# Query and key operands of the second attention block: turned first, split into three parts afterwards

## The chip, the cores and the metric

The kernel runs on one core of one Trainium2 chip. The metric is the time of one execution in microseconds (us) of device time; lower is better. The core has five engines with queues of their own, each worked off in order: TensorE (PE; its weight loads are shown as PEld), VectorE (DVE), ScalarE (ACT), GpSimd (POOL) and SyncE (SP, which issues DMAs here). They meet at semaphores only.

## The reference, cut to what matters

Two blocks of attention and a mixture of experts over x of shape (2, 2048, 128). The part that changes makes the operands of the second block's softmax attention:

```
xn = layernorm(x)
q = (xn @ wq.T).reshape(b, s, 16, 8);  k, v likewise
q = q * rsqrt(mean(q*q, -1) + 1e-6) * q_norm_w;   k likewise with k_norm_w
q, k = rope(q), rope(k)          # on the last 508 of 2048 positions
q = q / sqrt(8)
attn = softmax(q . k);  out = (attn @ v) @ wo.T
```

Next to it the second block's router is computed from the same xn: a softmax over 8 experts, the largest taken, and each token given a slot among the tokens sorted by expert.

## The kernel before, in words

The program is a row of stages, each a block at whose end all engines meet. The stage in question is `route_and_operands` (semaphores and buffers have the prefix `ro_`). In front of it stands a layer norm that leaves xn turned in `xnT`; behind it `sorted_experts` (`ffn_`), which needs the rows that this stage scattered; then `softmax_attention` (`at_`), whose queries and keys are loaded by DMA from what this stage leaves; then `finish`.

The stage has two halves that share the engines.

*Routing.* DVE works through a long row of small operations (L1069 to L1125), with one round trip to PE for counts (L984, L985) and one for a column sum (L987). At L1112 the slots are known; POOL then scatters 32 tiles of rows by indirect DMA (L945), and SP, which waits for all of them, loads the sorted rows (L938).

*Operands.* 4096 tokens in NG = 16 groups of 256 (TG = 2 tiles of 128). With tokens on the partitions, a group is projected (`project`, PE), its squares are taken (`square`, ACT L1007) and summed over each head (`statistics`, DVE L1133, L1135), the root is drawn (`take_root`, ACT L1016), inverted and multiplied in (`scale`, DVE L1140, L1142), groups 6, 7, 14 and 15 are rotated (`rope`, DVE L1152 to L1156), and each number is then split into three bfloat16 parts that add up to it: `first` (ACT, a copy to bfloat16), `remainder` (DVE L1160), `second` (ACT), `third` (DVE L1164). Attention wants features on the partitions, so the parts are turned by PE: `turn` (L975) makes 12 transposes of 128x128 bfloat16 for a group, 6 for queries and 6 for keys, into one PSUM bank each. `take` copies them out: queries by ACT, keys by ACT and DVE in turn. To have both plain and weighted projections the moving operand is `wqk`, 512 columns: the q and k weights, and the same times the norm weights.

The order on each engine is written by hand. PE: for g, `project(g + 2)`, then `turn(g)`, which waits for `lo` of the group (`third`), and for the bank that `take` of the group before must have emptied. ACT and DVE run loops over g in which group g is begun while groups g-1, g-2 and g-3 are at their later steps:

```
for g in range(NG + 3):          # ACT
    square(g); second(g - 2); take_values(g); first(g - 1); take_root(g); take(g - 3)
for g in range(NG + 3):          # DVE
    statistics(g); third(g - 2); scale(g); rope(g); remainder(g - 1); take(g - 3)
```

Buffers are rings of R = 3. `take_values` copies the value projection out of its bank; `project(g + 2)` waits for it and for `scale(g)`.

Of the kernel before, what the change touches and what calls it, by code (L numbers as in the profile page):

```python
# [11 lines left out]
P = 128  # L12
# [846 lines left out]

def load_rows(k, eng, U, pair, i, done):  # L860

    to = (k.queries, k.keys)[i][pair % 2]
    b, p = divmod(pair, PAIRS)
    for h in range(2):
        of = slice(2 * DK * p + DK * h, 2 * DK * p + DK * (h + 1))
        for place, part in PLACES[i]:
            at = h * HEAD_ROWS + place
            eng.dma_start(to[at:at + DK, :], U[i][of, part, b * SEQ:(b + 1) * SEQ]).then_inc(done, 16)
        if i == 0:

            at = h * HEAD_ROWS + SHIFT
            eng.dma_start(to[at:at + PARTS, :], k.zeros[0:PARTS, :].bitcast(BF16)).then_inc(done, 16)

def route_and_operands(k, w, bg, rows, r, sorted_dram, slots_of, U, V):

    nc = k.nc
# [6 lines left out]
    R = 3  # L886
    QK = 2 * D
    with ExitStack() as ctx:
# [14 lines left out]
        wqk = sb("wqk", [P, 2 * QK])  # L903
        norm = sb("norm", [P, QK])
        qk = sb("qk", [P, R, TG, QK])

        rest = sb("rest", [P, R, TG, QK])
        parts = sb("parts", [P, R, PARTS, TG, QK], BF16)
        rot = sb("rot", [P, 4, TG, 2 * HEADS, DK // 2])
# [4 lines left out]
        (weights_step, weights_made, projected, squared, summed, stat, rooted, inverted, scaled, v_out, rope_step, roped, hi, rest_out,  # L914
         mid, lo, turned, taken_q, taken_k_act, taken_k_dve) = (
            sem(n) for n in ("weights_step", "weights_made", "projected", "squared", "summed", "stat", "rooted", "inverted", "scaled",
                             "v_out", "rope_step", "roped", "hi", "rest_out", "mid", "lo", "turned", "taken_q", "taken_k_act",
                             "taken_k_dve"))
# [8 lines left out]
        weighted = lambda g: bank[:, first_bank(g):first_bank(g) + TG, QK:2 * QK]  # L927
# [20 lines left out]
        @block.tensor  # L948
        def _(pe):
            k.wait_late(pe)  # L950

            def project(g):
                if g >= 2:
                    pe.wait_ge(scaled, g - 1)
                    pe.wait_ge(v_out, g - 1)
                for t in range(TG):
                    at = g * COLS + t * P
                    nc.tensor.matmul(bank[:, first_bank(g) + t, :], xnT[:, at:at + P], wqk[:, :], start=True, stop=True)  # L958
                    mm = nc.tensor.matmul(bank[:, first_bank(g) + V_BANK, t * P:(t + 1) * P], xnT[:, at:at + P], w.wqkv[:, QK:3 * D],  # L959
                                          start=True, stop=True)  # L960
# [24 lines left out]
            nc.tensor.matmul(bank[:, COUNT_BANK, NW:2 * NW], k.ones[:, :], flat, start=True, stop=True).then_inc(counted, 1)  # L985
            pe.wait_ge(sum_ready, 1)
# [6 lines left out]
        def take_parts(copy, g, i):  # L993
            return copy(U[i][:, :, g * COLS:(g + 1) * COLS],
                        bank[:, T_BANK + i, :].bitcast(BF16)[:, 0:PARTS * COLS].rearrange("p (j t) -> p j t", j=PARTS))

        @block.scalar
        def _(act):
# [4 lines left out]
            def square(g):  # L1003
                act.wait_ge(projected, g + 1)
                if g >= R:
                    act.wait_ge(lo, g - R + 1)
                nc.scalar.activation(rest[:, g % R], plain(g), ACT.Square).then_inc(squared, 1)  # L1007
# [10 lines left out]
            def first(g):  # L1018
                act.wait_ge(scaled, g + 1)
                if turns(g):  # L1020
                    act.wait_ge(roped, turned_until(g))
                if g >= R:
                    act.wait_ge(turned, 2 * (g - R + 1))
                copy(parts[:, g % R, 0], qk[:, g % R]).then_inc(hi, 1)

            def second(g):
                act.wait_ge(rest_out, g + 1)
                copy(parts[:, g % R, 1], rest[:, g % R]).then_inc(mid, 1)

            def take(g):  # L1030
                act.wait_ge(turned, 2 * g + 1)
                take_parts(copy, g, 0).then_inc(taken_q, 1)
                if g % 2:
                    act.wait_ge(turned, 2 * g + 2)
                    take_parts(copy, g, 1).then_inc(taken_k_act, 1)

            for g in range(NG + 3):
                if g < NG:
                    square(g)
                if 2 <= g < NG + 2:  # L1040
                    second(g - 2)
                if g < NG:
                    take_values(g)
                if 1 <= g <= NG:
                    first(g - 1)
                if g < NG:
                    take_root(g)
                if g >= 3:
                    take(g - 3)

        @block.vector
        def _(dve):
# [18 lines left out]
            for i, scale in enumerate((DK ** -0.5, 1.0)):  # L1071
                ts(norm[:, i * D:(i + 1) * D].rearrange("p (h e) -> p h e", e=DK),
                   bc(w.norm_w[:, i, :].unsqueeze(1), [P, HEADS, DK]), scale, None, ALU.mult).then_inc(weights_step, 1)
# [53 lines left out]

            steps = 0

            def statistics(g):  # L1130
                dve.wait_ge(squared, g + 1)
                total = st[:, g % R, 0]
                red(total, by_head(rest[:, g % R]), X_AXIS, ALU.add).then_inc(summed, 1)  # L1133
# [3 lines left out]
            def scale(g):  # L1137
# [4 lines left out]
                tt(by_head(qk[:, g % R]), by_head(weighted(g)), bc(rstd.unsqueeze(3), [P, TG, 2 * HEADS, DK]), ALU.mult).then_inc(scaled, 1)  # L1142

            def rope(g):
                nonlocal steps
                dve.wait_ge(scaled, g + 1)
                a = by_head(qk[:, g % R])
                x0, x1 = a[:, :, :, 0:DK:2], a[:, :, :, 1:DK:2]
                at = g % ROPED * TG
                cos, sin = (bc(f[:, at:at + TG, :].unsqueeze(2), [P, TG, 2 * HEADS, DK // 2]) for f in (w.cos, w.sin))  # L1150
                for m, (x, f) in enumerate(((x0, cos), (x1, sin), (x0, sin), (x1, cos))):
                    tt(rot[:, m], x, f, ALU.mult).then_inc(rope_step, 1)  # L1152
                steps += 4
                dve.wait_ge(rope_step, steps)
                tt(x0, rot[:, 0], rot[:, 1], ALU.subtract)
                tt(x1, rot[:, 2], rot[:, 3], ALU.add).then_inc(roped, 1)  # L1156

            def remainder(g):
                dve.wait_ge(hi, g + 1)
                tt(rest[:, g % R], qk[:, g % R], parts[:, g % R, 0], ALU.subtract).then_inc(rest_out, 1)  # L1160

            def third(g):
                dve.wait_ge(mid, g + 1)
                tt(parts[:, g % R, 2], rest[:, g % R], parts[:, g % R, 1], ALU.subtract).then_inc(lo, 1)  # L1164

            def take(g):
                if g % 2 == 0:
                    dve.wait_ge(turned, 2 * g + 2)
                    take_parts(cp, g, 1).then_inc(taken_k_dve, 1)

            for g in range(NG + 3):
                if g < NG:
                    statistics(g)
                if 2 <= g < NG + 2:
                    third(g - 2)
                if g < NG:
                    scale(g)
                    if turns(g):
                        rope(g)
                if 1 <= g <= NG:  # L1180
                    remainder(g - 1)
                if g >= 3:
                    take(g - 3)
# [530 lines left out]
def build(nc, a, out):  # L1714

    with ExitStack() as whole:
# [144 lines left out]
        U = [sb(whole, n, [P, PARTS, TOK], BF16) for n in ("query_parts", "key_parts")]  # L1861
# [41 lines left out]
```

## Time and the profile before

| | |
|---|---|
| Median of 3 runs | 1983.7 us (1981.62 to 1983.73) |
| The profiled execution | 1984.38 us |
| Its span, first to last instruction | 1982.3 us |
| Mean granted TensorE clock | 0.927 of 2.4 GHz |
| Stage `route_and_operands` | 419 to 574 us of the span |
| `sorted_experts` and the start of attention | 574 to 720 us |
| Softmax attention | to 1961 us |

The profile covers one execution. "Granted clock" is the share of TensorE's full speed that the throttle allowed in a stretch. In a timeline, a line is a start, a length, the engine, the line of the kernel, the operation and, in brackets, the idle time of the engine ahead of it and what ended that.

### The profile page before, as it was taken

To read this page: it belongs to the slowest core of one execution; us is meant where nothing else is said; L and a number is where in the kernel's file an instruction comes from. 1 tells how busy PE (TensorE), PEld (TensorE's weight loads), DVE (VectorE), ACT (ScalarE), POOL (GpSimd) and SP (SyncE) were. 2 spreads that over 40 slices of the span, in tenths; PEclk is the share of its full clock that TensorE was granted. 3 is DMA by queue.
4 is the path that set the end of the run, shared out by engine and by line. 5 is a ranking of instruction groups with operands and counts; after the bars stand their busy time and mean duration, and the time that the engine had idled before them with its cause. 6 is when DMAs were issued, how large, how long until landed. Compare 5 with 4: busy or idle time off the path is not lost. (4 is left out here: it accounts for less than half of the span.)

```text
span 1982.3 us, 41860 instructions
## 1 busy us (share of the span) xinstructions
PE 1718.6 (87%) x16109; PEld 717.3 (36%) x16109; DVE 1591.2 (80%) x2845; ACT 1440.3 (73%) x2873; POOL 318.5 (16%) x668
## 2 busy tenths in 40 slices
PE   4883879465669999999999999999999999999997
PEld 4453653253359422222222222222222222222224
DVE  3751435755373799999999999999999999999982
ACT  2111547423335289999999999999999999999997
POOL 2272007525030000000000000000000000002221
PEclk9896998657669699999999999999999999999998
DMA  8014111313003001010010110100101101001001
GB/s 257 17 53 113 49 49 53 92 34 86 0 2 68 18 1 18 2 18 9 11 18 1 18 18 2 18 10 10 18 3 17 18 2 18 13 6 25 16 13 52
DMA packets 64294, 61.83 MB, mean 31 GB/s; under 512 B 10752, under 2 KB 52736, under 8 KB 64096
## 3 DMA queue, kind: packets, MB, share of 16 engines
q1 hardware_dynamic: 57952, 46.56, 10.5%
q0 software_dynamic: 6144, 12.60, 2.1%
q8 instruction: 128, 2.10, 0.5%
q14 instruction: 70, 0.57, 0.1%
HBM read 23.21 MB, written 22.94 MB: 23 GB/s over the span
## 5 line engine op out<-in xcount | busy, mean ns | idle before, releaser
L1631 DVE TENSOR_REDUCE at_tops<-bank 128x1 f32<-128x512 f32 x2048 | 1234.1, 683 | 16.3 <-PE bank L1489 10.5
L1590 ACT ACTIVATE experts_then_probs<-bank 128x512 f32<-128x512 f32 x2048 | 1093.4, 600 | 75.6 <-PE bank L1509 54.9
L1509 PE MATMUL bank<-queries,keys 64*128 64x512 bf16 x2048 | 631.4, 383 | 45.3 <-ACT experts_then_probs L1590 38.4
L1489 PE MATMUL bank<-keys,queries 64*128 64x512 bf16 x2048 | 656.7, 389 | 4.9 <-POOL at_shift L1402 4.3
L1525 PE MATMUL bank<-experts_then_probs,values 128*32 128x256 f32 x8192 | 642.1, 391 | 0.0
L1509 PEld LDWEIGHTS bank<-queries,keys 64*128 64x128 bf16 x2048 | 128.4, 93 | 503.5 <-ACT experts_then_probs L1590 412.0
L1525 PEld LDWEIGHTS bank<-experts_then_probs,values 128*32 128x32 f32 x8192 | 167.9, 108 | 311.3 <-ACT experts_then_probs L1590 207.5
L1421 POOL CAST at_shift<-at_neg 128x8 bf16<-128x8 f32 x64 | 13.9, 217 | 1112.9 <-DVE at_neg L1636 1112.9
L1489 PEld LDWEIGHTS bank<-keys,queries 64*128 64x128 bf16 x2048 | 148.5, 93 | 65.7 <-DVE at_tops L1631 50.3
L653 DVE COPY ep_weights<-WB 128x642 f32 x72 | 35.8, 497 | 88.9 <-DVE ep_slots L664 46.6
L1582 ACT ACTIVATE queries<-bank 3x512 bf16<-3x512 bf16 x128 | 75.4, 589 | 32.8 <-PE bank L1499 29.5
L680 ACT ACTIVATE ep_hT<-bank,ep_weights 128x128 f32<-128x128 f32 x144 | 45.1, 365 | 48.8 <-PE bank L622 48.7
L287 POOL DMA_INDIRECT sorted_pairs<-g_rows,pair_slot x64 | 62.4, 975 | 51.3 <-DVE pair_slot L534 32.1
L1007 ACT ACTIVATE ro_rest<-bank 128x512 f32<-128x512 f32 x16 | 9.5, 596 | 81.6 <-PE bank L959 81.6
L622 PE MATMUL bank<-ep_slotsT,ep_weights 128*128 128x128 f32 x288 | 51.8, 304 | 19.3 <-DVE ep_weights L653 19.3
L975 PE MATMUL bank<-identb,ro_parts 128*128 128x128 bf16 x192 | 23.5, 294 | 51.8 <-ACT query_parts L999 38.8
L958 PE MATMUL bank<-ro_wqk,xnT 128*128 128x512 f32 x64 | 56.2, 976 | 6.9 <-DVE ro_qk L1142 4.3
L1133 DVE TENSOR_REDUCE ro_st<-ro_rest 128x64 f32<-128x512 f32 x16 | 11.0, 685 | 61.8 <-ACT ro_rest L1007 61.8
L1287 DVE COPY ffn_w<-experts_then_probs 128x512 f32 x39 | 23.2, 594 | 40.6 <-PE bank L1253 37.6
L814 DVE RECIPROCAL qg_den<-qg_den 128x512 f32<-128x512 f32 x8 | 26.8, 3353 | 34.4 <-ACT qg_den L783 34.4
L717 POOL DMA_INDIRECT g_rows<-made_of_pairs,pair_slot x32 | 31.0, 969 | 141.8 <-SPq L698 132.4
L622 PEld LDWEIGHTS bank<-ep_slotsT,ep_weights 128*128 128x128 f32 x288 | 38.4, 194 | 31.3 <-DVE ep_weights L653 29.7
(252 smaller groups left out, 1597.1 us busy)
## 6 DMA issues: line engine op xcount, KB each, us to landing
queries<-query_parts SPq DMA_DIRECT2D x192, 32.0 KB
keys<-key_parts SPq DMA_DIRECT2D x192, 32.0 KB
sorted_pairs<-zeros SPq DMA_DIRECT2D x16, 288.0 KB, 3.3
ep_slots<-sorted_pairs SPq DMA_DIRECT2D x6, 768.0 KB, 9.2
made_of_pairs<-ep_slots SPq DMA_DIRECT2D x6, 768.0 KB, 4.1
sorted_tokens<-zeros SPq DMA_DIRECT2D x8, 312.0 KB, 3.4
x<-in_L_attn_x_dram SPq DMA_DIRECT2D x4, 512.0 KB, 6.0
experts_then_probs<-in_L_ffn_W_dram SPq DMA_DIRECT2D x1, 2048.0 KB, 10.0
```

Of the source, the lines that this page charges most:

```text
L287: pool.indirect_dma_start(sorted_dram, bass.IndirectOffsetOnAxis(ap=r0.slot[i][:, t:t + 1], axis=0), rows[:, t, :], None).then_inc(scatter ...
L622: mm = nc.tensor.matmul(bank[:, H_BANK + u, i * P:(i + 1) * P], wt[:, u, i * P:(i + 1) * P], slotsT[:, j // TPC % TR, j % TPC * P:(j % TPC ...
L653: nc.vector.tensor_copy(wt[:, j % R, :], WB[:, bass.ds(at, STRIDE0)]).then_inc(w_ready, 1)
L680: nc.scalar.activation(hT[:, u, i * P:(i + 1) * P], bank[:, H_BANK + u, i * P:(i + 1) * P], ACT.Relu, bias=wt[:, u, B1_AT + i:B1_AT + i + ...
L717: pool.indirect_dma_start(y[i][:, t, :], None, made_dram, bass.IndirectOffsetOnAxis(ap=r0.slot[i][:, t:t + 1], axis=0)).then_inc(gathered[ ...
L958: nc.tensor.matmul(bank[:, first_bank(g) + t, :], xnT[:, at:at + P], wqk[:, :], start=True, stop=True)
L1489: mm = nc.tensor.matmul(bank[:, unit_bank(u) + a % WIDE, :], queries[pair % 2][rows, at:at + P], keys[pair % 2][rows, kb * CHUNK:(kb + 1) ...
L1509: nc.tensor.matmul(bank[:, bank_of("score", n, s), :], keys[pair % 2][rows, at:at + P], queries[pair % 2][rows, c * CHUNK:(c + 1) * CHUNK] ...
L1525: mm = nc.tensor.matmul(bank[32 * j:32 * j + 32, O_BANK, 0:HALF], values[pair % 2][:, kt, h, :], probs[:, s % PR, q * HALF:(q + 1) * HALF] ...
L1582: nc.scalar.activation(queries[pair % 2][rows, c * CHUNK:(c + 1) * CHUNK], bank[rows, bank_of("shifts", m), 0:HALF].bitcast(BF16), ACT.Cop ...
L1590: nc.scalar.activation(probs[:, s % PR, :], bank[:, bank_of("score", n, s), :], ACT.Exp).then_inc(p_ready, 1)
L1631: nc.vector.tensor_reduce(tops[:, m % 2, h * TPC + qt, kb // WIDE:kb // WIDE + 1], bank[:, at:at + WIDE, :].rearrange("p b n -> p (b n)"), ...
```

## The change

Only `route_and_operands` changes, and with it the layout of its result: queries and keys now share one tensor `U` of [128, 2, 3, 4096].

The step order in a group becomes: project, scale, rope, then **turn**, and the split behind it. `turn(g)` makes 4 transposes of 128x128 float32 into one bank (two banks in turn); `first`, `remainder`, `second`, `third` work on turned numbers and write straight into U, so that `take` is gone. After turning, the norm weight of a feature is one number per partition: `of_row`, [128, 2]. In groups without rotation it is multiplied in by `first` (two ACT copies of 128x256 with a scale operand) and by `remainder` (two DVE scalar_tensor_tensor of 128x256); in rotated groups it is multiplied into the cosines and sines once, in eight small DVE products (`factors`), and `rope` runs on queries and keys apart (eight products and four sums of 128x128 elements in place of four and two of 128x256). `of_row` is made by two PE transposes behind `project(0)` and `project(1)` and two DVE copies, for which DVE waits (`norm_turned`) ahead of the router's operations. The weights `wqk` and their two DVE operations are gone; the moving operand has 256 columns. PE now runs `turn(g)` ahead of `project(g + 2)`. Rings are of R = 2.

```diff
-            eng.dma_start(to[at:at + DK, :], U[i][of, part, b * SEQ:(b + 1) * SEQ]).then_inc(done, 16)
+            eng.dma_start(to[at:at + DK, :], U[of, i, part, b * SEQ:(b + 1) * SEQ]).then_inc(done, 16)
...
-    R = 3
+    R = 2
...
-                    nc.tensor.matmul(bank[:, first_bank(g) + t, :], xnT[:, at:at + P], wqk[:, :], start=True, stop=True)
+                    nc.tensor.matmul(bank[:, first_bank(g) + t, 0:QK], xnT[:, at:at + P], w.wqkv[:, 0:QK], start=True, stop=True)
...
             def turn(g):
-                pe.wait_ge(lo, g + 1)
-                for i in range(2):
-                    if g and i == 0:
-                        pe.wait_ge(taken_q, g)
-                    if g and i == 1:
-                        pe.wait_ge(taken_k_dve if g % 2 else taken_k_act, (g + 1) // 2)
-                    out = bank[:, T_BANK + i, :].bitcast(BF16)
-                    for part in range(PARTS):
-                        for t in range(TG):
-                            at = (part * TG + t) * P
-                            mm = nc.tensor.transpose(out[:, at:at + P], parts[:, g % R, part, t, i * D:(i + 1) * D], k.identb[:, :])
-                    mm.then_inc(turned, 1)
+                pe.wait_ge(scaled, g + 1)
+                if turns(g):
+                    pe.wait_ge(roped, turned_until(g))
+                if g >= 2:
+                    pe.wait_ge(hi, g - 1)
+                    pe.wait_ge(rest_out, g - 1)
+                for t in range(TG):
+                    for i in range(2):
+                        mm = nc.tensor.transpose(turned_bank(g)[:, i, t * P:(t + 1) * P], qk[:, g % R, t, i * D:(i + 1) * D], k.ident[:, :])
+                mm.then_inc(turned, 1)
...
-            pe.wait_ge(weights_made, 2)
             project(0)
             project(1)
+            pe.wait_ge(norm_made, 2)
+            for i in range(2):
+                mm = nc.tensor.transpose(bank[:, SUM_BANK, i * P:(i + 1) * P], norm[:, i * D:(i + 1) * D], k.ident[:, :])
+            mm.then_inc(norm_turned, 1)
...
             for g in range(NG):
+                turn(g)
                 if g + 2 < NG:
                     project(g + 2)
-                turn(g)
...
             def first(g):
+                act.wait_ge(turned, g + 1)
+                if turns(g):
+                    copy(of_part(g, 0), turned_bank(g)).then_inc(hi, 1)
+                else:
+                    act.wait_ge(row_step, 2)
+                    for i in range(2):
+                        ins = nc.scalar.activation(of_part(g, 0)[:, i], turned_bank(g)[:, i], ACT.Copy, scale=of_row[:, i:i + 1])
+                    ins.then_inc(hi, 1)
...
+            square(0)
+            take_values(0)
+            take_root(0)
+            for g in range(NG):
+                if g + 1 < NG:
+                    square(g + 1)
+                first(g)
+                if g + 1 < NG:
+                    take_root(g + 1)
+                second(g)
+                if g + 1 < NG:
+                    take_values(g + 1)
...
-            cp(wqk[:, 0:QK], w.wqkv[:, 0:QK]).then_inc(weights_made, 1)
-            dve.wait_ge(weights_step, 2)
-            tt(wqk[:, QK:2 * QK], w.wqkv[:, 0:QK], norm[:, :], ALU.mult).then_inc(weights_made, 1)
+            dve.wait_ge(norm_turned, 1)
+            for i in range(2):
+                cp(of_row[:, i:i + 1], bank[:, SUM_BANK, i * P:i * P + 1]).then_inc(row_step, 1)
...
+                    for m, f in enumerate((w.cos, w.sin)):
+                        tt(factors[:, i, 2 * odd + m], f[:, :, :], of, ALU.mult).then_inc(row_step, 1)
...
             def remainder(g):
                 dve.wait_ge(hi, g + 1)
-                tt(rest[:, g % R], qk[:, g % R], parts[:, g % R, 0], ALU.subtract).then_inc(rest_out, 1)
+                if g >= R:
+                    dve.wait_ge(lo, g - R + 1)
+                if turns(g):
+                    tt(rest[:, g % R], turned_bank(g), of_part(g, 0), ALU.subtract).then_inc(rest_out, 1)
+                else:
+                    for i in range(2):
+                        ins = nc.vector.scalar_tensor_tensor(rest[:, g % R, i], turned_bank(g)[:, i], of_row[:, i:i + 1], of_part(g, 0)[:, i],
+                                                             ALU.mult, ALU.subtract)
+                    ins.then_inc(rest_out, 1)
...
+            statistics(0)
+            scale(0)
+            for g in range(NG):
+                if g + 1 < NG:
+                    statistics(g + 1)
+                remainder(g)
+                if g + 1 < NG:
+                    scale(g + 1)
+                    if turns(g + 1):
+                        rope(g + 1)
+                third(g)
```

## Rows read from the trace of the kernel before

**Rows 1.** Busy time by stretch (PE, PEld, DVE, ACT, POOL; clock; DMA), the groups.

```profile
441.40:574.00 132.60, 76.98 (x304) 45.62 (x304) 65.20 (x129) 49.21 (x102) 28.51 (x29) 0.68 0.12 34
```

**Rows 2.** Waits from 418 to 575 us: total, times, longest.

```profile
ACT ro_rest L1007 <- PE bank L959: 81.6, 15, 9.2
```

**Rows 3.** Timeline of one group, 514 to 523 us.

```profile
514.63 2.02 PE L958 MATMUL bank<-ro_wqk,xnT 128*128 128x512 f32 x2
...
519.23 0.60 ACT L1007 ACTIVATE ro_rest<-bank 128x512 f32<-128x512 f32 x1 [6.95 <-PE bank L959]
...
520.69 0.69 DVE L1164 TENSOR_TENSOR ro_parts<-ro_rest,ro_parts 128x512 bf16<-128x512 f32 x1
...
521.17 0.81 ACT L999 ACTIVATE query_parts<-bank 128x768 bf16<-128x768 bf16 x1
...
522.13 1.43 PE L975 MATMUL bank<-identb,ro_parts 128*128 128x128 bf16 x12 [2.93 <-ACT query_parts L999]
```

**Rows 4.** Instructions by line and form, 418 to 575 us: busy us, mean ns.

```profile
L1142 DVE TENSOR_TENSOR ro_qk<-bank,ro_st 128x512 f32<-128x512 f32 x16 | 11.1, 692 | 0.6
...
L999 ACT ACTIVATE ro_parts<-ro_rest 128x512 bf16<-128x512 f32 x16 | 10.0, 622 | 3.5 <-DVE ro_rest L1160 3.5
...
L1140 DVE RECIPROCAL ro_st<-ro_st 128x64 f32<-128x64 f32 x16 | 8.8, 553 | 0.6 <-ACT ro_st L1016 0.6
...
L999 ACT ACTIVATE attention_values<-bank 128x256 f32<-128x256 f32 x16 | 6.0, 376 | 0.0
...
L1152 DVE TENSOR_TENSOR ro_rot<-ro_qk,cos 128x256 f32<-128x256 f32 x8 | 3.4, 422 | 0.1
...
L1096 DVE TENSOR_TENSOR ro_counts<-ro_counts 128x128 f32<-128x128 f32 x1 | 0.3, 285 | 0.0
```

**Rows 5.** Instructions by line and form of other stages, whole span.

```profile
L789 ACT ACTIVATE g_rows<-g_rows,pair_gate 128x128 f32<-128x128 f32 x32 | 10.2, 397 | 23.5 <-DMA second_rows<-made_of_pairs,pair_slot 23.5
...
L824 DVE SCALAR_TENSOR_TENSOR g_rows<-second_rows,pair_gate,g_rows 128x128 f32<-128x128 f32 x32 | 9.1, 346 | 1.1 <-ACT g_rows L789 1.1
...
L1309 ACT ACTIVATE g_rows<-bank 128x128 f32<-128x128 f32 x32 | 8.9, 277 | 10.7 <-PE bank L1253 10.7
```

**Rows 6.** Timeline of the same two lines, four in a row.

```profile
379.52 1.28 ACT L789 ACTIVATE g_rows<-g_rows,pair_gate 128x128 f32<-128x128 f32 x4 [7.76 <-DMA second_rows<-made_of_pairs,pair_slot]
379.95 1.23 DVE L824 SCALAR_TENSOR_TENSOR g_rows<-second_rows,pair_gate,g_rows 128x128 f32<-128x128 f32 x4 [1.05 <-ACT g_rows L789]
```

**Rows 7.** Timeline of the stage's start, 418 to 444 us.

```profile
421.14 0.42 DVE L1081 TENSOR_REDUCE ro_one<-ro_probs 128x32 f32<-128x256 f32 x1
...
421.34 2.05 PE L958 MATMUL bank<-ro_wqk,xnT 128*128 128x512 f32 x2 [2.60 <-DVE ro_wqk L1079]
...
426.88 1.28 ACT L1016 ACT_TABLE_LOAD   x1
...
429.55 0.42 DVE L1092 COPY ro_counts<-bank 128x256 f32<-128x256 f32 x1 [4.85 <-PE bank L985]
...
441.38 0.68 DVE L1133 TENSOR_REDUCE ro_st<-ro_rest 128x64 f32<-128x512 f32 x1
...
443.34 0.69 DVE L1142 TENSOR_TENSOR ro_qk<-bank,ro_st 128x512 f32<-128x512 f32 x1
```

**Rows 8.** Timeline: rotation, the stage's end, float32 transposes of the stage behind.

```profile
557.38 0.75 DVE L1152 TENSOR_TENSOR ro_rot<-ro_qk,sin 128x256 f32<-128x256 f32 x2
...
573.01 0.80 ACT L999 ACTIVATE key_parts<-bank 128x768 bf16<-128x768 bf16 x1
...
594.93 1.06 PE L1231 MATMUL bank<-ident,g_rows 128*128 128x128 f32 x4
603.78 0.60 PE L1231 MATMUL bank<-ident,g_rows 128*128 128x128 f32 x4
```

**Rows 9.** Timeline of SP's queue: the last load of sorted rows.

```profile
483.99 1.29 SPq L938 DMA_DIRECT2D more_slots<-sorted_tokens  x1
```

**Rows 10.** DMA issues, 478 to 500 us: KB each, us to landing.

```profile
g_rows<-sorted_tokens SPq DMA_DIRECT2D x1, 384.0 KB, 8.7
```

More of the change, by code:

```diff
@@ L913, in route_and_operands @@
                              "slot_ready"))
[L914 to L918, printed above, removed]
+        (norm_made, norm_turned, row_step, projected, squared, summed, stat, rooted, inverted, scaled, v_out, rope_step, roped, turned, hi,
+         rest_out, mid, lo) = (
+            sem(n) for n in ("norm_made", "norm_turned", "row_step", "projected", "squared", "summed", "stat", "rooted", "inverted",
+                             "scaled", "v_out", "rope_step", "roped", "turned", "hi", "rest_out", "mid", "lo"))
         scattered = k.whole.enter_context(nc.semaphore("ro_scattered"))
@@ L1005, in square @@
                 if g >= R:
-                    act.wait_ge(lo, g - R + 1)
-                nc.scalar.activation(rest[:, g % R], plain(g), ACT.Square).then_inc(squared, 1)
+                    act.wait_ge(summed, g - R + 1)
+                nc.scalar.activation(squares[:, g % R], plain(g), ACT.Square).then_inc(squared, 1)
             def take_values(g):
@@ L1018, in first @@
             def first(g):
-                act.wait_ge(scaled, g + 1)
+                act.wait_ge(turned, g + 1)
                 if turns(g):
[L1021 to L1024, printed above, removed]
+                    copy(of_part(g, 0), turned_bank(g)).then_inc(hi, 1)
[4 more added lines that the diff above has]
+                    ins.then_inc(hi, 1)
             def second(g):
                 act.wait_ge(rest_out, g + 1)
[L1028 to L1049, printed above, removed]
+                copy(of_part(g, 1), rest[:, g % R]).then_inc(mid, 1)
+            square(0)
[10 more added lines that the diff above has]
+                    take_values(g + 1)
         @block.vector
@@ L1132, in statistics @@
                 total = st[:, g % R, 0]
-                red(total, by_head(rest[:, g % R]), X_AXIS, ALU.add).then_inc(summed, 1)
+                red(total, by_head(squares[:, g % R]), X_AXIS, ALU.add).then_inc(summed, 1)
                 dve.wait_ge(summed, g + 1)
@@ L1141, in scale @@
                 dve.wait_ge(inverted, g + 1)
-                tt(by_head(qk[:, g % R]), by_head(weighted(g)), bc(rstd.unsqueeze(3), [P, TG, 2 * HEADS, DK]), ALU.mult).then_inc(scaled, 1)
+                if g >= R:
+                    dve.wait_ge(turned, g - R + 1)
+                tt(by_head(qk[:, g % R]), by_head(plain(g)), bc(rstd.unsqueeze(3), [P, TG, 2 * HEADS, DK]), ALU.mult).then_inc(scaled, 1)
             def rope(g):
                 nonlocal steps
+                dve.wait_ge(row_step, 10)
@@ L1154, in rope @@
-                dve.wait_ge(rope_step, steps)
-                tt(x0, rot[:, 0], rot[:, 1], ALU.subtract)
-                tt(x1, rot[:, 2], rot[:, 3], ALU.add).then_inc(roped, 1)
+                for i in range(2):
+                    a = by_head(qk[:, g % R, :, i * D:(i + 1) * D])
+                    x0, x1 = a[:, :, :, 0:DK:2], a[:, :, :, 1:DK:2]
+                    cos0, sin0, cos1, sin1 = (bc(factors[:, i, m, at:at + TG, :].unsqueeze(2), [P, TG, HEADS, DK // 2]) for m in range(4))
+                    for m, (x, f) in enumerate(((x0, cos0), (x1, sin1), (x0, sin0), (x1, cos1))):
+                        tt(rot[:, m, i], x, f, ALU.mult).then_inc(rope_step, 1)
@@ L1158, in remainder @@
+                steps += 8
+                dve.wait_ge(rope_step, steps)
+                for i in range(2):
+                    a = by_head(qk[:, g % R, :, i * D:(i + 1) * D])
+                    tt(a[:, :, :, 0:DK:2], rot[:, 0, i], rot[:, 1, i], ALU.subtract)
+                    ins = tt(a[:, :, :, 1:DK:2], rot[:, 2, i], rot[:, 3, i], ALU.add)
+                ins.then_inc(roped, 1)
             def remainder(g):
                 dve.wait_ge(hi, g + 1)
-                tt(rest[:, g % R], qk[:, g % R], parts[:, g % R, 0], ALU.subtract).then_inc(rest_out, 1)
+                if g >= R:
+                    dve.wait_ge(lo, g - R + 1)
@@ L1163, in third @@
                 dve.wait_ge(mid, g + 1)
[L1164 to L1183, printed above, removed]
+                tt(of_part(g, 2), rest[:, g % R], of_part(g, 1), ALU.subtract).then_inc(lo, 1)
```

30 lines of the change are left out of this document (14 added, 16 removed).

## The prediction, made before the changed kernel ran

> **What bounds the kernel now.** I read the busy digits by slice first, to see which stage the edit lies in: from 720 us to 1961 us DVE and ACT are full in the softmax, which the change doesn't touch; the stage that it does touch has no full engine. Then busy time by stretch for the groups alone [rows 1]: of 132.6 us PE is busy 77, DVE 65, ACT 49, at a granted clock of 0.68, that is TensorE at its lower level (1.2 GHz) most of the time and at 2.4 GHz for the rest. 132.6 us for 16 groups is 8.3 us each, twice what the busiest of ACT and DVE needs. So it is a chain, and the waits say which [rows 2]: ACT waits 81.6 us for the projection. What PE waits for, one group shows, and the whole ring with it [rows 3].
>
> Projection from 514.63 to 519.2 (4.6 us for two tiles), square at 519.23, the head sums, `third` of the group two before at 520.69, then ACT's copy of the turned queries at 521.17; that frees the bank, for which PE had idled 2.93 us, the transposes start at 522.13 and take 1.43, and the next projection can only begin behind them. That is near 8.9 us in which every link waits for the link before: `lo` of a group stands behind the square of a group two later on DVE, that square stands behind its projection, and the transposes that wait for `lo` stand ahead of the next projection in PE's queue.
>
> The stage's end sets the start of the next one: ACT's last copy ends at 573.81 [rows 8], and the engines meet right behind. The other thing that the next stage needs, the sorted rows, was asked for at 483.99 to 485.28 [rows 9] and takes 8.7 us at most [rows 10], so it is there by 494. Until then some 80 us can be taken out of this stage before anything else ends last.
>
> **The change, part by part.**
>
> *The ring is cut.* `turn(g)` no longer waits for `lo` or for a copy, only for `scaled` (and `roped`), and for `first` and `remainder` of the group two before. What is left as a chain from `scaled(g)` to `scaled(g+1)`, through the queues as they are now written: `turn(g)` on PE, `first(g)` on ACT, `remainder(g)` on DVE, and behind it in DVE's queue the reciprocal and the multiplication of g+1. Each link:
> - `turn`: four float32 transposes of 128x128. The next stage does just that, in 1.06 us at the lower clock and 0.60 at the higher [rows 8]. The 12 bfloat16 ones took 1.43.
> - `first`: two ACT copies of 128x256 from PSUM with a scale operand, an operation that the trace doesn't have in this form. Without scale it is 376 ns [rows 4]. A 128x128 copy is 277 ns plain and 397 with scale (that one from SBUF) [rows 5], so 0 to 0.12 us more; I take all of it, 0.50 each. Four in a row took 1.28, so one starts 0.29 behind the last, 0.10 before it ends [rows 6]: 0.40 + 0.50 = 0.90 us.
> - `remainder`: two scalar_tensor_tensor of 128x256. At 128x128 it takes 346 ns [rows 5], 61 more than a tensor_tensor of that size at 285 [rows 4]; at 256 then 422 + 61 = 0.48, and from four in 1.23 us [rows 6] one holds DVE 0.05 less than that: 0.43 + 0.43 = 0.86. From below two plain 0.34 (0.68); from above, if its 346 ns grew by two cycles' worth of slope (0.27 us), 0.61 each, 1.2. I take 0.86, which is nearest to the row.
> - reciprocal 0.55 and `scale` 0.69 [rows 4], and four handovers between engines of some 0.04 us (the square at 519.23 behind a projection that ends at 519.2 [rows 3]): 0.16.
>
> Sum: 1.06 + 0.90 + 0.86 + 0.55 + 0.69 + 0.16 = **4.2 us** a group at the lower clock, 3.8 at the higher.
>
> The Trainium skill (ScalarE: Activation LUTs, What ACT_TABLE_LOAD costs) speaks against the scaled copy: each pointer operand adds about 93 ns to an ACTIVATE. The rows' 120 ns agree with it, if the source in SBUF makes the rest (as a copy of 512 from there takes 0.62, and the square from PSUM 0.60 [rows 3, 4]); by the page `first` would be 0.84, and the stage 0.7 us shorter, an estimate.
>
> *What must fit beside the chain.* PE: the moving operand shrinks from 640 to 384 columns a tile, so a group's projection from 4.6 us [rows 3] to 0.6 of it, 2.7, plus `turn` 1.06: 3.8 of 4.2 at the lower clock. DVE: head sums 0.9 (a reduction of 0.68 [rows 7] and a small operation), remainder 0.86, reciprocal 0.55, scale 0.69, `third` 0.69 [rows 3, 4]: 3.7. ACT: square 0.60, `first` 0.90, `second` 0.62, values 0.38 [rows 3, 4] and the small root: under 2.8. No engine is over 4.2, so none is the bound; the removed copies (0.81 of ACT for queries and as much for every second group's keys) and the bfloat16 transposes were cover, not chain, once the ring is cut. The head sums of g+1 run on DVE while PE and ACT turn and copy g (`third` and the sums 1.6 us, `turn` and `first` 1.96): hidden, so at nothing; were that cover gone, they would cost up to 0.9 a group. `third(g)` stands behind `scale(g+1)` and waits for `second(g)`, which ends 0.7 us behind `remainder`, before `scale` ends at 1.2: nothing.
>
> *Rotated groups (6, 7, 14, 15).* `rope` gets eight products and four sums of 128 elements. A tensor_tensor of 256 holds DVE 0.33 us (two in 0.75, the second's 0.42 taken off [rows 8]) and lasts 0.42, so one of 128, at 0.285 [rows 4], holds it some 0.20: 7 x 0.20 + 0.29 + 0.04 + 3 x 0.20 + 0.29 = 2.6 us. `first` and `remainder` are then single operations of 0.62 and 0.61 held (0.69 [rows 4]). From `scaled` of such a group to the next: 2.6 + 1.06 + 0.62 + 0.61 + 0.55 + 0.69 + 0.2 = 6.3 us.
>
> *The front.* The projections needn't wait for `wqk` any more: they can start behind the first logits operation, at about 419.7 in place of 421.34 [rows 7]. But DVE now waits at `norm_turned`, ahead of the whole routing row, for two tiles times two groups of projection (4 x 1.35 = 5.4 at the lower clock, as the first ones ran before) and two transposes (0.5): 425.6, then two copies of one column, 0.3. So L1081 moves from 421.14 to about 425.9. What hid it before: DVE then stood idle 4.85 us for the counts [rows 7], because PE was still projecting. That wait goes: the row up to `hot_ready` is 3.55 us (421.14 to 429.55 less 4.85), so 429.5, and the counts then take PE 2.0 us at the lower clock (128x512 takes 2.05 [rows 7], and this is two of 256): 431.5 in place of 429.55, 2.0 us late. At the higher clock it would be 0.3. The eight small products for the cosines add 0.8 in front of the groups. So the groups start 2.8 us later: `scaled(0)`, at 444.03 before [rows 7], comes at 446.8. The scatter and SP's loads, queued behind the slots, move 2 us late with it: to 496, under the next stage's start below, so at nothing.
>
> *The sum.* From `scaled(0)` to `scaled(15)`, 12 steps x 4.2 and 3 x 6.3 (out of groups 6, 7, 14) = 69.3; behind `scaled(15)` the last group's rope, turn, first, remainder, second, third: 2.6 + 1.06 + 0.62 + 0.69 + 0.62 + 0.69 + 0.2 = 6.5. Together 75.8 at the lower clock. The clock touches the chain in `turn` only (0.46 x 16 = 7.4 us if always high); with a mean of 0.68 between 0.5 and 1 it is high for 0.36 of the time: 2.7 off, 73.1 [rows 1, 8]. End at 446.8 + 73.1 = 519.9, say 520.0, in place of 573.8: **53.8 us less**, against the profiled execution's 1984.4 (0.7 over the median): 1930.6. With handovers a little longer than the one that I read: **1931 us**.
>
> Bounds: clock always high (4.7) and the front at 0.3 (1.7) take off 6.4 us, plain prices in `first` and `remainder` (0.24 + 0.18 in 12 groups) another 5: 1920. Clock always low adds 2.7, the remainder at 1.2 us 4, head sums that show in part (0.4 x 15) 6: 1944.
>
> **Rivals.**
> - *PE takes the chain's place.* It has 0.4 us a group to spare at the lower clock. If a narrow projection costs more than its columns say (each tile still loads weights four times), say 5.0 us a group on PE, 15 x 0.8 = 12 us are lost, more with rotated groups waiting: 1943 to 1955. For it: PE's share rises to nine tenths. Against: at the higher clock, which the stage behind has from 603.78 on [rows 8], it needs half.
> - *ACT reloads tables.* If a scaled copy didn't share a table with the root, two loads of 1.28 us [rows 7] a group would enter the chain: 15 x 2.6 = 38 lost, 1969. Against: four scaled copies take 1.28 us with nothing between them [rows 6], and one such load alone is as long.
> - *The saving is taken back behind.* The next stage would have to wait for something at a fixed time. Only the sorted rows are such; they come at 496, 24 us early. It decides if they came 54 us later; then no change, 1984.
> - *Slower: the groups run one behind the other.* With rings of two and `turn(g)` ahead of `project(g+2)`, the overlap hangs on PE having projected two groups ahead. If that lead is lost, a group is the whole row: projection 2.8, square 0.6, sums and root 1.2, reciprocal and `scale` 1.3, `turn` 1.1, `first` and `remainder` 1.8, `second` and `third` 1.4, about 10.2 us; it decides from 8.3. 16 x 10.2 and 4 x 2.1 for the rotation give 172, 39 us more than 132.6: 2023. Against: `project(g+2)` waits only for `scaled(g)` and `take_values(g)`, both done when `turn(g)` ends.
>
> **How the numbers follow.** The forecast has 0.81, PE as bound 0.09, tables 0.03, taken back 0.03, slower 0.04. The likeliest gives 1931; its bounds 1920 to 1944 hold about 0.8 of everything, and I leave the others outside. 0.2% of 1984 is 4 us, about what a measurement of this kernel can tell: faster 0.81 + 0.09 + 0.03 = 0.93, same 0.03, slower 0.04.
>
> **What would show it.** The stage ends near 520, the next starts there and lasts as before. Between two `scale` multiplications: 3.8 to 4.2 us without rotation, 6 with. `first`'s copies at 0.46 to 0.50 us, each remainder at 0.42 to 0.61, four transposes in 1.06 or 0.60. DVE idles some 5 us ahead of L1081 and little ahead of the counts. The prediction is wrong if PE has no idle time between groups, if table loads stand between copies and roots, or if a later stage got longer.

## The result, and the profile after

The changed kernel takes **1926.8 us** (median of 4 runs, 1925.29 to 1927.49) beside 1983.7 for the kernel before on the same chip (4 runs, 1981.62 to 1984.79): a ratio of 0.9715, 95% interval 0.9702 to 0.9728, or 56.9 us less. The forecast was 1931, with 1920 to 1944 as its range. The profiled execution has a span of 1923.6 us, 58.7 under that of before (1982.3).

First the busy time by stretch, as in [rows 1] but from the end of the first `scale` on: the groups without the last rotated pair, and that pair.

```profile
447.40:505.00 57.60, 32.72 (x168) 27.72 (x168) 52.12 (x120) 32.67 (x81) 25.93 (x27) 0.90 0.26 76
505.00:518.70 13.70, 2.18 (x8) 1.43 (x8) 10.87 (x34) 3.47 (x8) 0.00 (x0) 0.57 0.01 2
```

From the end of the first `scale` to the end of the stage, 129.8 us (444.03 to 573.81) have become 71.3 (447.42 to 518.69). PE still idles for two fifths of the first stretch, yet its granted clock is 0.90 there where it was 0.68. DVE is now busy 52 of 57.6 us. The forecast had it at 3.7 us of a step of 4.2, or of 3.8 at the higher clock, and said that no engine is the bound; so little room gave a theory of its own below.

One group, which answers to [rows 3]:

```profile
455.65 0.66 PE L974 MATMUL bank<-ident,ro_qk 128*128 128x128 f32 x4 [1.72 <-DVE ro_qk L1143]
...
456.15 0.60 PE L960 MATMUL bank<-wqkv,xnT 128*128 128x256 f32 x2
...
456.36 0.84 ACT L1024 ACTIVATE operand_parts<-bank,ro_of_row 128x256 bf16<-128x256 f32 x2 [0.52 <-PE bank L974]
...
457.23 0.88 DVE L1172 SCALAR_TENSOR_TENSOR ro_rest<-bank,ro_of_row,operand_parts 128x256 f32<-128x256 f32 x2 [0.20 <-ACT operand_parts L1024]
...
458.02 0.54 DVE L1139 RECIPROCAL ro_st<-ro_st 128x64 f32<-128x64 f32 x1
...
458.60 0.69 DVE L1143 TENSOR_TENSOR ro_qk<-bank,ro_st 128x512 f32<-128x512 f32 x1
...
459.34 0.66 PE L974 MATMUL bank<-ident,ro_qk 128*128 128x128 f32 x4 [1.71 <-DVE ro_qk L1143]
```

This is the chain of the forecast, link by link: turn, first, remainder, reciprocal, scale, turn. From one turn to the next it is 3.69 us: 0.71 + 0.87 + 0.79 + 0.58 + 0.74, each link counted to the start of the next one. The projection of the group two on lies beside it, and PE waits 1.7 us for `scale` where it had waited 2.93 for a copy of ACT's [rows 3].

The front of the stage and its end, beside [rows 7, 8]:

```profile
421.33 1.19 PE L960 MATMUL bank<-wqkv,xnT 128*128 128x256 f32 x2 [1.00 <-DVE ro_probs L1063]
...
425.21 0.60 PE L960 MATMUL bank<-wqkv,xnT 128*128 128x256 f32 x2
...
426.28 0.22 DVE L1072 COPY ro_of_row<-bank 128x1 f32<-128x1 f32 x2 [4.04 <-PE bank L982]
426.42 0.41 DVE L1074 TENSOR_REDUCE ro_one<-ro_probs 128x32 f32<-128x256 f32 x1
...
432.13 0.42 DVE L1085 COPY ro_counts<-bank 128x256 f32<-128x256 f32 x1 [2.17 <-PE bank L987]
...
446.73 0.69 DVE L1143 TENSOR_TENSOR ro_qk<-bank,ro_st 128x512 f32<-128x512 f32 x1
...
504.67 0.69 DVE L1143 TENSOR_TENSOR ro_qk<-bank,ro_st 128x512 f32<-128x512 f32 x1
...
505.46 1.70 DVE L1155 TENSOR_TENSOR ro_rot<-ro_qk,ro_factors 128x128 f32<-128x128 f32 x8
...
508.20 1.09 PE L974 MATMUL bank<-ident,ro_qk 128*128 128x128 f32 x4 [4.50 <-issue]
...
511.14 0.69 DVE L1143 TENSOR_TENSOR ro_qk<-bank,ro_st 128x512 f32<-128x512 f32 x1
...
518.00 0.69 DVE L1178 TENSOR_TENSOR operand_parts<-ro_rest,operand_parts 128x512 bf16<-128x512 f32 x1 [0.70 <-ACT operand_parts L998]
...
519.01 1.30 PE L1238 MATMUL bank<-ident,g_rows 128*128 128x128 f32 x5 [3.06 <-PEq L889]
```

DVE waits 4.04 us for the turned norm weights (L1072) ahead of the whole routing row, and 2.17 for the counts where it had waited 4.85 [rows 7]. The first rotated step that stands free of projections lasts 6.47 us between its two multiplications (504.67 to 511.14). The last operation of the stage ends at 518.69, and the next stage starts there.

Where the time went, read from the same three points of each timeline (the first DVE operation of the stage, the first and the last group's `scale`, and the first copy of `ffn_w` in the next stage):

| kernel | stage start to first scale | first to 16th scale | 16th scale to `ffn_w` |
|---|---|---|---|
| before | 24.30 | 120.63 | 10.88 |
| after | 26.11 | 64.41 | 8.60 |

That is +1.8, -56.2 and -2.3: -56.7 us for the stage, and the medians differ by 56.9. (The span's further 2 us are spread between executions: this stage starts 1.6 us later, and from the softmax's first maxima to the end it is 1314.8 us here, 1317.5 in the profile of the same kernel taken again below, and 1318.1 before.)

### The profile page after: what moved, and what is told of

Its sections match the earlier page's. It is cut to its first block and busy times, and to the rows that moved or that the text cites. A ratio compares the mean times of both kernels' runs of the same rounds, so it can differ in the third digit from the quotient of the medians.

```text
span 1923.6 us, 41668 instructions
## 1 busy us (share of the span) xinstructions
PE 1677.3 (87%) x15983; PEld 703.1 (37%) x15983; DVE 1590.5 (83%) x2881; ACT 1428.0 (74%) x2861; POOL 319.8 (17%) x668
## 5 line engine op out<-in xcount | busy, mean ns | idle before, releaser
L387 ACT ACTIVATE qT<-bank,bq 128x512 f32<-128x512 f32 x8 | 5.5, 687 | 58.3 <-PE bank L301 58.3
L1249 PE MATMUL bank<-xnT,ffn_w 128*128 128x128 f32 x312 | 44.4, 288 | 4.5 <-DVE ffn_w L1294 4.5
L425 DVE TENSOR_SCALAR kr_feat<-bank 128x512 f32<-128x512 f32 x64 | 40.2, 682 | 8.4 <-PE bank L320 8.3
L974 PE MATMUL bank<-ident,ro_qk 128*128 128x128 f32 x64 | 13.0, 339 | 38.6 <-DVE ro_qk L1143 21.0
```

Of the source, the lines that this page charges most:

```text
L425: ts(feat[:, u % RING, r, :], bank[:, F_BANK + r, :], 0.0, EPS, ALU.max, ALU.add).then_inc(feat_out, 1)
L1249: mm = nc.tensor.matmul(bank[:, H_BANK + u, i * P:(i + 1) * P], w1[:, u, i * P:(i + 1) * P], slotsT[:, at:at + P], start=True, stop=True)
```

## The experiments

Theory A was that of the forecast: what pays is that `turn` no longer waits for the split of its own group, so that projection, turn and split of different groups run side by side. Theory B: what pays is that there is less to do, fewer transposes, narrower projections and no copies of turned operands.

**The old kernel in another order.** Nothing of the change but PE's order: the kernel before, with each `turn` put behind the projection of one group more. All the old work stays.

```diff
-            for g in range(NG):
+            for g in range(NG + 1):
                 if g + 2 < NG:
                     project(g + 2)
-                turn(g)
+                if g:
+                    turn(g - 1)
```

> The kernel before with one thing changed: PE makes the transposes of a group one projection later. All its work stays: the projection of 512 columns, 12 bfloat16 transposes a group, the copies out. Theory A (order): the saving came from cutting the ring in which a projection waits for the transposes and the transposes for work behind that projection. Then a group takes its own engine's time: on PE 4.3 + 1.4 us at 1.2 GHz, some 3.7 at 2.4 GHz from the chain on DVE; the groups take 72 to 94 us in place of 130, and the time is 1926 to 1948 us, 1940 the likeliest. Theory B (work): it came from fewer transposes, narrower projections and no copies out. Then nothing is won here, or below 10 us: 1974 to 1984.

Measured: 1925.0 us (4 runs, 1923.72 to 1925.2), a ratio of 0.9709 (0.9693 to 0.9725) to the kernel before on that chip, 1983.0. The whole gain is there without any of the rest. A's figure was too slow: 1940 as the likeliest, 1926 as its lower bound. From its timeline:

```profile
458.09 0.69 DVE L1143 TENSOR_TENSOR ro_qk<-bank,ro_st 128x512 f32<-128x512 f32 x1
...
458.80 0.83 PE L975 MATMUL bank<-identb,ro_parts 128*128 128x128 bf16 x12
459.00 0.60 ACT L1008 ACTIVATE ro_rest<-bank 128x512 f32<-128x512 f32 x1 [0.29 <-PE bank L959]
...
459.63 0.69 DVE L1134 TENSOR_REDUCE ro_st<-ro_rest 128x64 f32<-128x512 f32 x1 [0.17 <-ACT ro_rest L1008]
...
461.67 0.69 DVE L1143 TENSOR_TENSOR ro_qk<-bank,ro_st 128x512 f32<-128x512 f32 x1
```

The square at L1008 waits 0.29 us for its projection where it had waited 6.95 [rows 3], the twelve bfloat16 transposes run with no wait ahead of them in this group (in every second group the second six wait 1.1 us for DVE's copy of the keys), and a group is 3.6 us from scale to scale. First to 16th scale is 64.28 us, the same as with the change. B falls as the cause.

Two things stay open here. The equal totals have different sources: in this kernel DVE hardly waits at all (six times between 452 and 500 us, 3.8 us in all, 2.7 of it once behind the rotated groups), so its own queue, with the key copies in it, looks like what a group comes down to, while in the changed kernel it is the chain; that they agree to 0.1 us is chance. And the clock rose with the new order, to 0.90 between 445 and 505 us. At the lower level PE needs some 4.6 + 1.4 = 6.0 us a group (an estimate from [rows 3]), which wouldn't fit into 3.6, so by that estimate part of the 58 us hangs on the clock; no run holds it low.

**The wide projection given back.** After, with the moving operand at 512 columns again (two copies of the 256 side by side; the second half is computed and read by nobody).

```diff
-  nc.tensor.matmul(bank[:, first_bank(g) + t, 0:QK], xnT[:, at:at + P], w.wqkv[:, 0:QK], ...)
+  nc.tensor.matmul(bank[:, first_bank(g) + t, :], xnT[:, at:at + P], wqk[:, :], ...)
```

> The changed kernel with the projection as wide as before: 512 columns for queries and keys, the second half of them read by nobody. Theory A (order): PE has the time beside the chain, 3.0 of 3.7 us at 2.4 GHz; at 1.2 GHz it would need 5.1 of 4.2. More columns keep PE busier, so the higher clock is likely: 1927, at most 1938. Theory B (work): the narrower projection is the largest piece of work saved, 1.8 us a group at 1.2 GHz, 0.9 at 2.4: 15 to 29 us more, 1942 to 1956.

Measured: 1929.6 us (4 runs, 1926.82 to 1930.28), ratio 0.9729 (0.9713 to 0.9746).

```profile
458.17 0.69 DVE L1148 TENSOR_TENSOR ro_qk<-bank,ro_st 128x512 f32<-128x512 f32 x1
...
458.92 0.65 PE L976 MATMUL bank<-ident,ro_qk 128*128 128x128 f32 x4 [1.00 <-DVE ro_qk L1148]
...
459.41 1.02 PE L962 MATMUL bank<-ro_wqk,xnT 128*128 128x512 f32 x2
...
461.85 0.69 DVE L1148 TENSOR_TENSOR ro_qk<-bank,ro_st 128x512 f32<-128x512 f32 x1
```

A projection of 512 columns takes 1.02 us for 0.60, PE's wait shrinks from 1.72 to 1.00, and the group is 3.68 us as before: first to 16th scale 64.63 against 64.41. At the clock that these groups had (0.87 between 447 and 505 us), the narrower operand is worth nothing in them; whether it would be at 1.2 GHz, where A has PE at 5.1 us in a step of 4.2, no run shows. What the run lost is at the front (29.19 us to the first scale for 26.11), where DVE waits 7.66 us behind these projections in place of 4.04.

**Turn and projection in the old sequence.** After, with `project(g + 2)` ahead of `turn(g)` again.

```diff
             for g in range(NG):
-                turn(g)
                 if g + 2 < NG:
                     project(g + 2)
+                turn(g)
```

> The changed kernel with PE's two steps in the old order: projection of the group two ahead first, then the transposes. Theory A (order): the projection enters the chain between scale and transposes, 1.3 us a group at 2.4 GHz, 2.6 at 1.2: 16 to 31 us more than the changed kernel, 1943 to 1958. Theory B (work): the work is the same, so 1927, within 3.

Measured: 1964.4 us (2 runs, 1963.53 and 1965.32), ratio 0.991 (0.989 to 0.993): two thirds of the gain gone, 6 us more than A's bound. Its stretch and one step:

```profile
447.00:534.00 87.00, 49.34 (x156) 39.20 (x156) 47.87 (x111) 28.97 (x73) 28.19 (x27) 0.50 0.18 51
```

```profile
468.11 1.22 PE L960 MATMUL bank<-wqkv,xnT 128*128 128x256 f32 x2 [3.02 <-DVE ro_qk L1143]
...
470.83 1.06 PE L974 MATMUL bank<-ident,ro_qk 128*128 128x128 f32 x4
...
474.92 1.22 PE L960 MATMUL bank<-wqkv,xnT 128*128 128x256 f32 x2 [3.02 <-DVE ro_qk L1143]
```

The projection is now a link of the chain: 2.72 us ahead of each turn (468.11 to 470.83), and behind it the 4.1 us that a step takes after at the lower clock; together 6.81. The granted clock is 0.50 throughout, 1.2 GHz, and at that level twelve such steps and three rotated ones of 6.5 make 101.2 us; from the first to the 16th scale it was 101.1, where 64.4 stood before the order was turned. A's bound was too low because it added the projection's 2.6 us at the lower level to steps of the changed kernel that had mostly run at the higher one: 3.7 us, where the rest of this step takes 4.1.

**A lead of one group.** After, with one group projected ahead in place of two: only `project(0)` in front, `project(g + 1)` behind `turn(g)`.

```diff
             project(0)
-            project(1)
...
                 turn(g)
-                if g + 2 < NG:
-                    project(g + 2)
+                if g + 1 < NG:
+                    project(g + 1)
```

> The changed kernel with PE projecting only one group ahead of the transposes in place of two. Theory A (order, with the lead of two as what keeps square, sums and root off the chain): projection, square, sums and root enter it, about 5.6 us a group at 2.4 GHz and 7.4 at 1.2 in place of 3.7 to 4.1: 29 to 49 us more than the changed kernel, 1956 to 1976. Theory B (work): 1927 to 1932.

Measured: 1975.9 us (6 runs, 1974.99 to 1978.18), ratio 0.9964 (0.9952 to 0.9976).

```profile
468.26 1.11 PE L974 MATMUL bank<-ident,ro_qk 128*128 128x128 f32 x4 [3.60 <-DVE ro_qk L1142]
...
469.17 1.06 PE L960 MATMUL bank<-wqkv,xnT 128*128 128x256 f32 x2
...
471.97 0.60 ACT L1005 ACTIVATE ro_squares<-bank 128x512 f32<-128x512 f32 x1 [4.01 <-PE bank L961]
472.47 0.83 ACT L1023 ACTIVATE operand_parts<-bank,ro_of_row 128x256 bf16<-128x256 f32 x2
...
473.43 0.87 DVE L1171 SCALAR_TENSOR_TENSOR ro_rest<-bank,ro_of_row,operand_parts 128x256 f32<-128x256 f32 x2
...
474.80 0.69 DVE L1142 TENSOR_TENSOR ro_qk<-bank,ro_st 128x512 f32<-128x512 f32 x1
...
475.54 1.12 PE L974 MATMUL bank<-ident,ro_qk 128*128 128x128 f32 x4 [3.60 <-DVE ro_qk L1142]
```

Turn of one group, then projection, square, head sums and `scale` of the next stand behind each other, with the turned group's `remainder` between sums and reciprocal: 7.28 us a step, near A's 7.4 for the lower clock, and 1975.9 us lies at A's upper bound. This is the new kernel with all its shorter work, and it is 0.4% faster than the kernel before. It is the mechanism of the slower rival, at a lower price (7.28 where it had 10.2, because `first` runs beside the head sums, and `second` and `third` run beside `scale` and turn) and therefore under its 8.3.

**What bounds a group now.** After the first four runs, a second question: DVE is busy nine tenths of the groups. Theory C said that it is DVE's queue that sets the 3.7 us; the forecast's chain says that DVE waits for `first`. One run shortens chain and DVE together: after, with the unrotated groups split by one plain copy and one subtraction, as the rotated ones are. It leaves the norm weight of those groups out of the output.

```diff
-                if turns(g):
+                if True:
                     copy(of_part(g, 0), turned_bank(g)).then_inc(hi, 1)
...
-                if turns(g):
+                if True:
                     tt(rest[:, g % R], turned_bank(g), of_part(g, 0), ALU.subtract).then_inc(rest_out, 1)
```

> The changed kernel without the norm weights in the groups that are not rotated: one copy and one subtraction of 128x512 there in place of two scaled copies and two scalar_tensor_tensor of 128x256. Chain alone: 0.24 us less on ACT and 0.27 on DVE in 12 groups, 6 us: 1921. DVE as what now bounds a group (it has 0.2 us of idle time in 3.7): only its 0.27 us and some of the idle time count, 3.3 to 4.6 us: 1922 to 1923.5. If neither sets the pace: 1927.

Another only DVE: the division by 8 and the epsilon move from a DVE operation into the scale and bias of ACT's root (its norm transposes stand in front, as in the last run below).

```diff
-                act.wait_ge(stat, g + 1)
-                nc.scalar.activation(st[:, g % R, 1], st[:, g % R, 0], ACT.Sqrt)...
+                act.wait_ge(summed, g + 1)
+                act.wait_ge(eps_ready, 1)
+                nc.scalar.activation(st[:, g % R, 1], st[:, g % R, 0], ACT.Sqrt, scale=1.0 / DK, bias=eps[:, :])...
...
-                dve.wait_ge(summed, g + 1)
-                ts(total, total, 1.0 / DK, EPS, ALU.mult, ALU.add).then_inc(stat, 1)
```

> The order of the run with the norm weights first, and one DVE operation a group less: the division by 8 and the epsilon go into the scale and bias of ACT's root. DVE as the bound: 0.15 us a group less, 2 us in all, on top of 4.3: 1920.5. If the chain through PE and ACT is the bound, the second part gives nothing: 1922.5.

And the changed kernel once more on that chip, to measure these against: 1925.9 us (5 runs, 1925.23 to 1927.61), ratio 0.9703 (0.969 to 0.9717) to 1984.7 before.

> The changed kernel as it is, on the chip of these runs: 1926.8 us, within 1.5.

The plain split gave 1923.0 us (5 runs, 1922.31 to 1924.81; 0.9691, 0.9678 to 0.9704), with its turns 3.26 us apart:

```profile
457.04 0.66 PE L974 MATMUL bank<-ident,ro_qk 128*128 128x128 f32 x4 [1.29 <-DVE ro_qk L1143]
...
457.74 0.60 ACT L998 ACTIVATE operand_parts<-bank 128x512 bf16<-128x512 f32 x1 [0.51 <-PE bank L974]
...
458.37 0.69 DVE L1169 TENSOR_TENSOR ro_rest<-bank,operand_parts 128x512 f32<-128x512 f32 x1
...
460.30 0.66 PE L974 MATMUL bank<-ident,ro_qk 128*128 128x128 f32 x4 [1.29 <-DVE ro_qk L1143]
```

0.43 us a group less: 0.87 to 0.63 for `first`, 0.79 to 0.61 for `remainder`, the 0.24 and 0.18 that the forecast's lower bound had. From first to 16th scale it is 59.9 us for 64.5; the medians show 2.9 of these 4.6. By its own expectation this run doesn't speak for the chain: 1923.0 lies where DVE sets the pace (1922 to 1923.5), the chain alone had 1921. It takes 0.42 us off the chain and 0.18 off DVE's work, and no wait of DVE is left ahead of the subtraction (L1169): the 0.20 us that DVE had to spare are used up, chain and DVE come out equal, and the run can't tell them apart.

The kernel without DVE's small operation gave 1922.2 us (5 runs, 1919.17 to 1924.6; 0.9682, 0.9668 to 0.9695), of which the front gives its part (next run, 1922.9). The expectations, 1922.5 and 1920.5, are closer together than its runs, so the time doesn't decide; the trace does. In the groups it gave nothing:

```profile
455.61 0.66 PE L977 MATMUL bank<-ident,ro_qk 128*128 128x128 f32 x4 [1.72 <-DVE ro_qk L1145]
...
457.18 0.88 DVE L1174 SCALAR_TENSOR_TENSOR ro_rest<-bank,ro_of_row,operand_parts 128x256 f32<-128x256 f32 x2 [0.43 <-ACT operand_parts L1028]
...
459.29 0.66 PE L977 MATMUL bank<-ident,ro_qk 128*128 128x128 f32 x4 [1.72 <-DVE ro_qk L1145]
```

The turns are 3.68 us apart, as in after, and the time saved on DVE stands ahead of the remainder as a wait for `first`, 0.43 us where it was 0.20. First to 16th scale: 64.56 us (64.54 in the changed kernel taken again). C falls for the changed kernel: the chain is the bound there, though DVE is only 0.2 us a group behind it.

**The wait at the front.** After, with the two transposes of the norm weights ahead of the projections in PE's queue.

```diff
-            project(0)
-            project(1)
             pe.wait_ge(norm_made, 2)
...
             mm.then_inc(norm_turned, 1)
+            project(0)
+            project(1)
```

> The changed kernel with the two transposes of the norm weights ahead of the first two projections on PE, so that DVE doesn't stand behind these projections ahead of the router's row. Theory (the front costs what the wait at the norm weights adds): DVE's 4.0 us of idle time ahead of that row go, the counts follow the projections at 2.4 GHz as they did before, and the first group's scale comes 4.3 us earlier: 1922.5 us against 1926.8. Rival: the wait only moves to the counts, which then stand behind the projections for longer; 1 to 2 us, 1925 to 1926.

Measured: 1922.9 us (5 runs, 1922.17 to 1924.57), ratio 0.9689 (0.9675 to 0.9702); its slowest run is under the fastest of the changed kernel beside it (1925.23).

```profile
422.52 0.66 PE L980 MATMUL bank<-ident,ro_norm 128*128 128x128 f32 x2 [1.27 <-DVE ro_norm L1065]
...
423.21 0.23 DVE L1072 COPY ro_of_row<-bank 128x1 f32<-128x1 f32 x2
423.64 0.42 DVE L1074 TENSOR_REDUCE ro_one<-ro_probs 128x32 f32<-128x256 f32 x1 [0.20 <-ACT ro_probs L1000]
...
428.42 0.42 DVE L1085 COPY ro_counts<-bank 128x256 f32<-128x256 f32 x1 [1.22 <-PE bank L987]
```

DVE's 4.04 us are gone and the counts wait 1.22. From the stage's start to the first scale it is 21.47 us, under the 24.30 of before; 4.6 to 5.6 less than the two profiles of the changed kernel (26.11 and 27.07), of which the medians show 3.0. The stage starts at another time in each profiled execution (418.9 to 421.8 us over all these kernels); whether the rest is that spread stays open. This version, with or without the small operation moved to ACT, is the fastest of those run that keep the output, and both beat the changed kernel by 3 us or more.

## Why the prediction was right

**What bounds it, and the cut of the ring: right.** The cause as the forecast gave it, a `turn` that stood behind its group's split and ahead of the next projection, is shown by the old kernel, which gains the same 58 us when the order alone is changed. (PE's own wait in [rows 3] ended with ACT's copy of the turned queries, which stands behind the same square as the split does; a later `turn` frees both, and no run separates them.) The new kernel loses 38 and 49 us when a projection is put back into its chain, by projection ahead of turn or by one group less of lead; neither is the old ring itself. What the forecast didn't see is that the rest of the change, turning first, float32 transposes, the narrow operand, isn't needed for the gain at the clock of these runs: the old work in the new order takes 3.6 us a group.

**The chain's price: right to 0.1 us a link.** 3.8 at the higher clock by the forecast, 3.69 measured (counting a handover of 0.04 with each, `turn` is 0.07 dearer, `first` 0.07 and `remainder` 0.1 cheaper, so the sum agrees partly because errors cancel); 4.2 at the lower, and the first two turns start 4.14 us apart (447.48 and 451.62). The two operations that no row had:

```profile
L1024 ACT ACTIVATE operand_parts<-bank,ro_of_row 128x256 bf16<-128x256 f32 x24 | 10.1, 471 | 7.6 <-PE bank L974 7.5
...
L1172 DVE SCALAR_TENSOR_TENSOR ro_rest<-bank,ro_of_row,operand_parts 128x256 f32<-128x256 f32 x24 | 10.5, 479 | 3.3 <-ACT operand_parts L1024 3.2
```

In these groups by line and form, the remainder is at 479 ns where the forecast had 0.48, and the scaled copy at 471 where it had 500. Two of the copies last 0.84 us, for 0.90 in the sum. The plain copy of that size was 376 [rows 4], so the scale costs 95 ns. The Trainium skill (ScalarE: Activation LUTs, What ACT_TABLE_LOAD costs) puts a pointer operand at about 93 ns, and the trace agrees with that rather than with the 120 that the forecast took from a copy out of SBUF.

**The rotated step: 0.2 short.** 6.3 forecast, 6.47 measured; from the end of the last `scale` (511.83) to the end of the stage 6.9 for 6.5.

**The front: right at the lower clock.** 2.8 us forecast; 2.8 in the changed kernel taken again (27.07 less 24.30), where all early projections ran at 1.2 GHz, and 1.8 in the profile shown, where the clock rose at the last of them (L960 at 425.21, 0.60 us).

**The clock: the term that was mis-sized.** The forecast let the higher level stand for 0.36 of the time, the old share, and came to 73.1 us from the end of the first scale (447.42) to the end of the stage; measured 71.3. The granted clock was 0.90 over all but the last pair of groups. With a step half as long, PE's pauses were shorter (1.7 us for 2.93) and the clock was higher; the old share shouldn't have been taken as given (the rows on it stand in the last section; no run shows the cause by itself). The error was small, because the clock touches one link in five. Put the measured mean of the 71.3 us, 0.84, into the forecast's own sum and it comes to 70.8; the rotated steps and the end, 0.9 over their price, bring it to 71.7. So the 1.8 us here and the 1.0 at the front, both on the same side, are nearly all by which the stage came out under the forecast (56.7 us less, for 53.8).

**The rivals.** PE as the bound: refuted for the clock that the groups had by the wide projection, which took 0.72 us of PE's wait a group and no time. Tables: two loads in the stage, as before, and none between groups. Taken back behind: from the first copy of `ffn_w` to the softmax's first maxima it is 89.1 us (519.74 to 608.83), before 89.3. Slower: not in the change, but its mechanism is real, as the lead of one shows.

## What to carry to other kernels

When a wait closes a ring through several queues, write the ring down and first try the one line that opens it, in the old kernel: here moving a `turn` by one group was worth all that a rewrite of the stage was worth. A busy share of nine tenths doesn't by itself make an engine the bound; take a little work off it alone, and see whether the step gets shorter or a wait grows by as much. And look at what a new small operand is queued behind: the two norm transposes cost 3 us because they stood behind projections that nobody needed yet.

## What the runs showed of the hardware

The same busy share of TensorE went with two different granted clocks. In the groups of the changed kernel PE was busy 32.72 of 57.6 us, a share of 0.57, in pieces with 1.7 us of idle time between them, at a granted clock of 0.90.
